# One graph-network kernel: the first layer of the next group moved to the end of a step, the scatter split around the second layer, and every VectorE comparison written in rows

## What is computed

```
h = relu(layernorm(x))
m = mlp3([h[src], h[dst], edge_attr])      # per edge: 320 -> 256 -> 256 -> 128, relu between
s = segment_sum(m, src) + segment_sum(m, dst)
x = x + mlp3([h, s, attention(h)])         # per node
h = relu(layernorm(x))
x = x + gelu(gcn(h, src, dst))             # x @ W, normalised by degree, with self loops
```

## Time and profile before

| what | value |
|---|---|
| median of 3 runs | 766.12 us |
| profiled execution | 766.94 us, its span 765.2 us |
| PE busy in the span | 737.4 us |
| DVE busy | 697.7 us |
| ACT busy | 646.7 us |
| POOL busy | 539.4 us |
| start of step 1, 2, 3 on PE (first L627 product) | 47.42, 63.65, 74.89 us |
| start of step 61, of step 63 and of the node network on PE | 699.74, 721.68, 734.88 us |
| mean granted clock of PE | 0.993 |

### The profile page before, as it was taken

How to read it: one execution, slowest core, us unless ns; L and a number is a source line. 1 busy time by engine, 2 the same in 40 slices (tenths; PEclk the granted TensorE clock), 3 DMA queues, 4 the chain that set the end, 5 groups by cost and what they waited for, 6 DMA issues and landing times.

```text
span 765.2 us, 13420 instructions
## 1 busy us (share of the span) xinstructions
PE 737.4 (96%) x4171; PEld 621.8 (81%) x4171; DVE 697.7 (91%) x1477; ACT 646.7 (85%) x819; POOL 539.4 (70%) x530
## 2 busy tenths in 40 slices
PE   7589999999999999999999999999999999999997
PEld 6468888888878888888878888888878888888865
DVE  7779999999999999999999999999999999997676
ACT  5557988899879988899888888898879888898744
POOL 3677777777777777777777777777777777777000
PEclk9989999999999999999999999999999999999999
DMA  7534334444434433434344434444344434443000
GB/s 228 164 114 133 120 113 128 126 125 130 119 116 127 129 116 114 132 119 133 107 132 125 123 109 121 132 131 124 112 125 126 133 114 118 124 131 96 16 1 29
DMA packets 42567, 90.17 MB, mean 118 GB/s; under 512 B 11136, under 2 KB 17920, under 8 KB 42496
## 3 DMA queue, kind: packets, MB, share of 16 engines
q0 software_dynamic: 24576, 67.14, 29.1%
q1 hardware_dynamic: 17920, 22.16, 9.9%
HBM read 86.64 MB, written 2.62 MB: 117 GB/s over the span
## 4 chain that ended last, share of the span: by engine, by line
PE 85%; DVE 5%; POOL 3%; issue 3%; ACT 2%; DMA 1%; DVEq 1%; SPq 0%; POOLq 0%
PE bank L657 29%; PE bank L627 20%; PE bank L637 14%; PE bank L609 7%; PE bank L603 7%; PE bank L671 4%; POOL rows_sb L470 2%; POOL rows_sb L478 1%; PE bank L756 1%; PE bank L800 1%; DVE oh_key L1146 1%; DMA table_a<-rows_sb 1%; DVE oh_low L1145 1%; ACT dist L874 1%; DMA rows_sb<-table_b,ends_i 1%
## 5 line engine op out<-in xcount | busy, mean ns | idle before, releaser
L470 POOL DMA_INDIRECT rows_sb<-table_a,ends_i x256 | 271.5, 1061 | 83.4 <-issue 77.7
L478 POOL DMA_INDIRECT rows_sb<-table_b,ends_i x256 | 260.8, 1019 | 78.0 <-issue 78.0
L874 ACT ACTIVATE dist<-iota_h,neg_mid 128x1024 f16<-128x1024 f16 (+1 forms) x256 | 293.7, 1149 | 0.0
L1089 DVE TENSOR_SCALAR ring<-dist,half_gap,times 128x1026 fp32r<-128x1026 f16 (+1 forms) x194 | 222.5, 1147 | 4.9 <-ACT dist L874 4.8
L657 PE MATMUL bank<-ring,m_hi 128*128 128x512 f32 x504 | 169.7, 418 | 0.0
L657 PE MATMUL bank<-ring,m_lo 128*128 128x512 f32 x504 | 159.0, 397 | 0.0
L627 PE MATMUL bank<-ring,w_hi 128*128 128x512 f32 x512 | 149.8, 394 | 2.8 <-DVE ring L1069 2.8
L859 ACT ACTIVATE h_sb<-bank,b_sb 128x512 f32<-128x512 f32 x128 | 87.5, 684 | 69.2 <-PE bank L627 69.2
L1146 DVE TENSOR_SCALAR oh_key<-iota_h,key_f,minus_base 128x258 bf16<-128x258 f16 x321 | 128.4, 400 | 0.1
L637 PE MATMUL bank<-w_sb,h_sb 128*128 128x128 f32 x1024 | 125.0, 275 | 0.1
L609 PE MATMUL bank<-ident,rows_sb 128*128 128x128 f32 x512 | 112.7, 277 | 8.8 <-DVE rows_sb L1137 8.8
(11 more groups left out here) (189 smaller groups left out, 795.0 us busy)
## 6 DMA issues: line engine op xcount, KB each, us to landing
e_raw<-edge_attr_t SPq DMA_DIRECT2D x128, 128.0 KB, 3.1
rows_sb<-table_a,ends_i POOLq DMA_INDIRECT x256, 2.8
rows_sb<-table_b,ends_i POOLq DMA_INDIRECT x256, 2.9
table_a<-rows_sb SPq DMA_DIRECT2D x4, 256.0 KB, 3.6
table_b<-rows_sb SPq DMA_DIRECT2D x4, 256.0 KB
x_sb<-x SPq DMA_DIRECT2D x2, 256.0 KB, 3.3
out<-oh_key SPq DMA_DIRECT2D x4, 128.0 KB, 1.8
u_sb<-uW SPq DMA_DIRECT2D x1, 384.0 KB, 5.0
```

Of the source, the lines that this page charges most:

```text
L470: nc.gpsimd.indirect_dma_start(got[:, b, t, 0, :], None, table_a, bass.IndirectOffsetOnAxis(ap=ends_i[:, 0, tile:tile + 1], axis=0),).then ...
L478: nc.gpsimd.indirect_dma_start(got[:, b, t, 1, :], None, table_b, bass.IndirectOffsetOnAxis(ap=ends_i[:, 1, tile:tile + 1], axis=0),).then ...
L874: nc.scalar.activation(to, of, ACT.Abs, bias=neg_mid[:, bass.ds(g * GT + t, 1)]).then_inc(dist_ready, 1)
L1089: nc.vector.tensor_scalar(to, of, half_gap[:, tile], times[:, tile], ALU.is_equal, ALU.mult).then_inc(inc_ready, 1)
```

## The change

- **PE**: a step begins with tiles 0 and 1 of the scatter of group g - 1, then the second layer of group g, tiles 2 and 3 of the scatter, the messages of g, and last both halves of the first layer of group g + 1, with the count products between its transposes.
- **Counts**: half h is made by DVE and multiplied by PE in step h; no step has two. The last half is counted in step 63, and `sum_counts`, `count_ends` and `degrees` come after it. The bias of the sums is added after each half of the last scatter.
- **DVE**: a step begins with both `low_first` of group g and, in every even step from 2, `window_out`; then the three comparisons of group g with the one-hots between them, then the two halves of `add_pairs` (now `add_pair`) for group g + 1, with the last one-hot between, `low_messages` and `low_edges` (L1063, the low part of edge attributes).
- **Rows**: tile 1 is compared in rows as well, and `distance` writes it so. The special case of the last two groups is gone.
- **ACT**: a step begins with `last_gap` and `last_incidence` of group g - 1; distances 0 to 2 of group g + 1 are made in step g.
- **Before the steps**: PE runs 12 and then 6 products that nothing uses (`keep_busy`), and the arithmetic on the ends of edges (`middles`) is moved and split.

```
-    IN_ROWS = (0, 2)
+    IN_ROWS = (0, 1, 2)
...
-        TWICE = (16, 33, 48)
...
         def counted_in(g):
 
-            first = g + sum(g > x for x in TWICE)
-            found = (first, first + 1) if g in TWICE else (first,)
-            return [h for h in found if 0 <= h < HALVES]
-
-        def made_in(g):
-
-            return counted_in(g + 1)
+            return g if 0 <= g < HALVES else None
...
                 if g == GROUPS:
-                    add_bias_of_sums()
                     last_scatter(g - 1, 1 - b)
                     return
+                if past:
+                    for t in range(GT // 2 if nxt else GT):
+                        scatter(g - 1, 1 - b, t)
                 if now:
                     second_layer(g, b, 0)
                     second_layer(g, b, 1)
+                if past and nxt:
+                    for t in range(GT // 2, GT):
+                        scatter(g - 1, 1 - b, t)
+                if now and not nxt:
+                    for j in range(HALF):
+                        count_tile(counted_in(g), j)
+                if now:
+                    messages(g)
                 if nxt:
                     first_layer(g + 1, 1 - b, i + b, 0, counted_in(g))
-                if past:
-                    scatter(g - 1, 1 - b, 0)
-                if nxt:
                     first_layer(g + 1, 1 - b, i + b, 1, counted_in(g))
-                if now:
-                    messages(g)
-                if past:
-                    scatter(g - 1, 1 - b, 1)
-                    scatter(g - 1, 1 - b, 2)
-                if g == LAST_SUM + 1:
+                else:
                     count_ends()
-                if past:
-                    scatter(g - 1, 1 - b, 3)
-
-
+
+
+            keep_busy(WARM)
             pe.wait_ge(rows_ready, 1)
             more_windows()
+            keep_busy(WARM // 2)
             pe.wait_ge(uh_ready, KH * NH)
             pe.wait_ge(w_lo_ready, 4)
...
-                if makes and exists(g):
-                    h = makes[0]
+                h = counted_in(g)
+                if now:
+                    low_first(g, b, 0)
+                    low_first(g, b, 1)
+                if is_first(g):
+                    middles_done()
+                    low_edges(1, 1)
+                if now and summed_in(g - 1) is not None:
+                    window_out(summed_in(g - 1))
+                if now:
                     tile0 = window_tile(h // 2)
-                    one_hots(h, tile0, (0, 1))
-                if past:
-                    incidence(g - 1, 1)
-                if nxt:
-                    add_pairs(g + 1)
-                if makes and exists(g):
-                    one_hots(h, tile0, (2,))
-                if past:
-                    incidence(g - 1, 2)
-                if past and all_on_vector(g - 1):
-                    incidence(g - 1, 3)
-                if exists(g + 2):
-                    low_edges(g + 2, b)
-                if g == FIRST + 1:
-                    middles_done()
-                if nxt:
-                    low_first(g + 1, 1 - b, 0)
-                if makes and exists(g):
-                    one_hots(h, tile0, (3,))
-                if nxt:
-                    low_first(g + 1, 1 - b, 1)
-                if makes and exists(g):
-                    one_hots(h, tile0, (4,))
+                if now and not nxt:
+                    one_hots(h, tile0, range(HALF))
                 if now:
                     incidence(g, 0)
+                if now and nxt:
+                    one_hots(h, tile0, (0,))
+                if now:
+                    incidence(g, 1)
+                if now and nxt:
+                    one_hots(h, tile0, (1, 2, 3))
+                if now:
+                    incidence(g, 2)
+                if nxt:
+                    add_pair(g + 1, 0)
+                if now and nxt:
+                    one_hots(h, tile0, (4,))
+                if nxt:
+                    add_pair(g + 1, 1)
+                if now and not nxt:
+                    window_out(summed_in(g))
+                    sum_counts()
+                if now:
                     low_messages(g, b)
-                for more in makes[1 if exists(g) else 0:]:
-                    one_hots(more, window_tile(more // 2), range(HALF))
-                if summed_in(g) is not None:
-                    window_out(summed_in(g))
-
-            def add_pairs(g):
+                if now and exists(g + 2):
+                    low_edges(g + 2, b)
+                if now and not nxt:
+                    degrees()
+                if nxt and not now:
+                    middles_scaled()
+
+            def add_pair(g, half):
 
```

More of the change, by code:

```diff
@@ L610, in first_layer @@
                                           start=False, stop=True, is_transpose=True, skip_group_check=True)
-                    if counting and t in COUNTS_AT[k]:
-                        count_tile(counting[0], t + k * len(COUNTS_AT[0]))
+                    if counting is not None and t in COUNTS_AT[k]:
+                        count_tile(counting, t + k * len(COUNTS_AT[0]))
                 mm.then_inc(z1t_psum, 1)
[L614 to L617, removed]
             def second_layer(g, b, m):
@@ L905, in group @@
                 now, nxt, past = exists(g), exists(g + 1), exists(g - 1)
+                if past:
+                    last_gap(g - 1)
+                    last_incidence(g - 1)
                 if exists(g + 2):
                     round_edges(g + 2, b, i + 1)
-                if past:
-                    distance(g - 1, 2)
                 if now:
+                    if not nxt:
+                        distance(g, 3)
                     relu_second(g, 0)
-                if past:
-                    distance(g - 1, 3)
+                    if nxt:
+                        distance(g, 3)
+                    relu_second(g, 1)
+                if now and nxt:
+                    distance(g + 1, 0)
+                    distance(g + 1, 1)
                 if now:
-                    relu_second(g, 1)
-                if past and not all_on_vector(g - 1):
-                    last_gap(g - 1)
+                    high_messages(g, b)
+                if now and nxt:
+                    distance(g + 1, 2)
                 if nxt:
                     relu_first(g + 1, 1 - b, 0)
-                if past and not all_on_vector(g - 1):
-                    last_incidence(g - 1)
-                if nxt:
                     relu_first(g + 1, 1 - b, 1)
-                if now:
-                    distance(g, 0)
-                    high_messages(g, b)
-                    distance(g, 1)
+                if nxt and not now:
+                    for t in range(DT):
+                        distance(g + 1, t)
             act.wait_ge(dve_step, 2)
@@ new lines, in group @@
+                if now:
+                    low_messages(g, b)
+                if now and exists(g + 2):
+                    low_edges(g + 2, b)
+                if now and not nxt:
+                    degrees()
+                if nxt and not now:
+                    middles_scaled()
+            def add_pair(g, half):
+                b, n = g % GB, g // GB
+                tiles = slice(2 * half, 2 * half + 2)
+                for t in (2 * half, 2 * half + 1):
+                    dve.wait_ge(ga_done[b][t], 16 * (n + 1))
+                    dve.wait_ge(gb_done[b][t], 16 * (n + 1))
+                nc.vector.tensor_tensor(got[:, b, tiles, 0, :], got[:, b, tiles, 0, :], got[:, b, tiles, 1, :],
+                                        ALU.add).then_inc(pair_added, 1)
```

56 lines of the change are left out of this document (21 added, 35 removed).

## The result

The changed kernel takes 777.17 us (median; 775.97 to 777.92), the kernel before 766.42 beside it: a ratio of 1.0138, 95% interval 1.0119 to 1.0157. It is slower by 10.75 us; 6.8 were forecast, and 777.2 lies in the forecast's own range. Medians and ratios here leave out executions over 1.5% above the fastest of their kernel: 1235.31 us of the kernel before, 1240.01 with the sums last, 773.86 and 775.98 with tile 2 plain. The profiled execution took 775.97 us with a span of 774.2.

The account below looks back on a forecast made before the run. TensorE was taken to bound the kernel before, VectorE's loop the even steps after. The terms -7.6 - 4.5 + 2.4 + 16.5 = +6.8 us gave 773.7 us profiled, 772.9 median; own range 768 to 779, whole range 759 to 782.

Parts of the forecast that it names:

- VectorE's chain bounds the even step: Even steps: the loop through VectorE and TensorE takes 11.24 us against TensorE's 10.64; +16.5 us in all.
- The size of the wait: TensorE between second and third transpose of even steps: 0.60 us summed, 0.55 taken, thirty steps, +16.5 us.
- The doubled steps: Three steps with two halves of counts, each 2.52 us over a plain step, become plain: -7.6 us.
- The start: First steps: step 1 5.6 us shorter, step 0 3 longer, products ahead 1.9 off; -4.5 us, ends -7 and -1.
- the added products: Products in front of the steps keep TensorE busy and take an estimated 1.9 us off the start of step 0.
- The end: Steps 61 to 63 and last scatter: 35.14 us become 37.5, +2.4 us (0 to +4).
- By load alone VectorE has nothing to give: VectorE over two steps: 21.1 us of work against TensorE's 21.28, so almost no room.
- The second layer has 0.1 us of cover left after an even step: Second layer: two scatter tiles cover 1.9 us, the work takes 1.6, VectorE is 0.15 late; 0.1 us is left.
- Gathers at nothing: GpSimd's gathers in the later steps cost nothing; if late, VectorE's adds would show a wait for a transfer.
- TensorE as the bound: Rival: even step's loop is 0.4 us shorter or more, wait 0 to 0.25 us, time 756.4 to 764; chance 0.21.
- Cancelling: Rival: an even-step wait of about 0.32 us gives 766.1 us within 1.5; chance 0.12.
- The slower one: Rival: adds meeting gathers and compares of 1.36 us make the wait 0.8 to 1.07, time 780.4 to 788.2; chance 0.12.

Follow-up runs that it names:

- the sums last: Changed kernel with the two reductions of the window's counts moved to the end of VectorE's step: 767.63 us, ratio 1.0022 to the kernel before.
- tile 2 plain: Changed kernel with incidence tile 2 compared as one plain row, tiles 0 and 1 in rows: 763.38 us, ratio 0.9960 to the kernel before.
- the sums behind the adds: Changed kernel with incidence tile 1 as one plain row and the window's two reductions right behind the second add: 757.71 us, ratio 0.9899 to the kernel before.
- tile 1 plain: Changed kernel with incidence tile 1 compared as one plain row, tiles 0 and 2 in rows: 760.55 us, ratio 0.9927 to the kernel before.
- the reductions last besides: Changed kernel with incidence tile 1 as one plain row and the window's two reductions at the end of VectorE's step: 767.23 us, ratio 1.0018 to the kernel before.

## Why the prediction was right, point by point

- *VectorE's chain bounds the even step.* Right, place and mechanism: the waits are in front of a transpose and of a count beside it, in even steps alone, released by VectorE; shortening the chain by 0.53 shortens the step by 0.53.
- *The size of the wait* is the term of the sum that was mis-sized. The links summed to 0.60; 0.05 was then taken off for modelled ends, and 0.62 was measured. It doesn't all lie between the second and the third transpose, as forecast, but about half of it at the count between the first and the second. Thirty steps make 18.6 us in place of 16.5. A few longer steps give the rest (step 30 has 11.49, some odd ones 10.68).
- *The doubled steps*, -7.6: gone, as said.
- *The start*, -4.5: step 3 begins at 69.82 us in place of 74.89, -5.1. The wait of the earlier trace rows is gone and step 1 is 5.6 shorter, as forecast. The other two terms were off: of the 1.9 us for the added products no run shows more than 0.6 (without them step 0 begins at 37.50 in place of 36.87), and step 0 is 1.7 longer (10.92, 9.25), not 3. Step 0 begins 1.3 us earlier, and step 1 0.4 later (47.79, 47.42) where +1.1 was forecast; that the sum came near is in part luck.
- *The end*, +2.4: 38.29 against 35.14 is +3.15, of which 0.62 is step 62's wait, counted with the even steps: +2.5.
- Together, on the profiled spans: -7.6 - 5.1 + 18.6 + 2.5 = 8.4, with 0.6 for longer steps 9.0 (774.2 - 765.2). Between the medians it is 10.75: the profiled execution was the shortest of its kernel, and that of before lay 0.5 above its median.
- *By load alone VectorE has nothing to give.* The sum of 21.1 us for two steps was low, 21.52 is measured (21.89 from `low_first` at 321.64 to 343.53, less 0.37 of gaps). But the load of two steps wasn't the limit: with the sums last VectorE stands in odd steps, and with 0.53 us less work in each step the odd step is the same. It was a second chain, from `low_messages` to `low_first`, which VectorE's even step and the messages feed within 0.05 us of each other.
- *The second layer has 0.1 us of cover left after an even step.* Too tight: with the sums last `low_first` came 0.70 later than in an even step and the step grew by 0.33, so some 0.37 was there; the 0.37 by which it is later with the sums behind the adds cost 0.02.
- *Gathers at nothing.* Right for this kernel; they fell from 1061 and 1019 ns to 968 and 963 in the mean. By the page "SBUF — State Buffer" of the Trainium skill, section "Who interferes with whom", a VectorE instruction with two inputs in SBUF contends with a GpSimd instruction that reads SBUF, and the lock on the ports they share is exclusive; so an add could stand for a whole gather. On that side the trace doesn't agree: the adds keep their 0.60. On the other side it does: gathers issued in an add take 1.22 in the mean where most take 0.95. With a plain compare ahead of the adds that gets a price: in the profiled execution with tile 2 plain, the three odd steps of 12.0 to 12.6 us are 4.7 us together.
- *Rivals.* TensorE as the bound (756.4 to 764) needed a loop 0.4 us shorter: the kernels at 757 to 761 have one, by their edits. Cancelling would have needed 0.32 us of wait. The slower one named compares of 1.36 and adds that gathers hold up; no compare passed 1.26 from start to start, and the adds kept their 0.60. The 0.85 that the prediction gives for the plain one was read at one that met a gather; with tile 1 plain 61 of 64 take 0.72, so that rows cost 0.53 and not 0.40.

## What to carry to other kernels

When an instruction of a second engine moves to the end of that engine's step, add up the whole loop through both engines, link by link, and compare it with the bound engine's step: here 11.24 was computed and 11.26 measured. Two edits that use the same slack must be priced together: alone they were worth -5.7 and +6.3 us, together +10.75. Work that is to be hidden belongs where its engine waits for something that comes at a fixed time, and not behind that wait: the reductions, 0.86 us, cost 0.33 in an odd step behind `low_messages` and 0.02 ahead of it.

## What the runs showed of the hardware

What VectorE does while a gather is issued sets the gather's time. Counted over the gathers of the changed kernel: issued in an add (two inputs in SBUF) 27, mean 1.22 us; in a compare in rows 183, mean 0.95; in `low_first`, `low_messages` or a one-hot 0.95. With tile 1 plain: in the plain compare 58, mean 1.21; in `low_edges` 56, mean 1.08.

Where in the instruction the gather is issued counts as well. All 26 gathers that an add lengthened in the changed kernel end 0.82 us after the add's end: one issued 0.01 us into an add took 1.48 us, one issued 0.49 into it 1.01. With tile 1 plain the 57 that the plain compare lengthened end 0.81 to 0.83 us after the compare's end. With the reductions last besides, 27 of 29 gathers fall within 0.02 us of the plain compare's start, and these take 0.95. A gather issued in a one-hot just ahead of an add is held too, up to 1.57 us with tile 1 plain.

So the compare in rows, which is 0.53 us slower on VectorE, leaves GpSimd alone (all but 1 of 183), and the plain one holds it up; what the rows are worth depends on which of the two engines has room.
